# Graph network stack, layer 0: head 0's operands turned on TensorE, part of the adjacency tiles and values moved into the tile loop

## What is computed

```
h = relu(layernorm(x)); Q, K, V = h@Qw+Qb, h@Kw+Kb, h@Vw+Vb        # 512 columns each
S1 = einsum('id,kdh->ikh', Q, A1); S2 = einsum('jd,kdh->jkh', K, A2)
e = S1[i, adj[i,j]] + S2[j, adj[i,j]]                               # per head
attn = softmax(leaky_relu(e, 0.2), axis=1)
x = x + (einsum('ijh,jhd->ihd', attn, V per head).reshape(n, 512) @ Pw + Pb)
```

## Time and profile before

| | before |
|---|---|
| median of 3 runs | 1069.88 us (1066.89 to 1075.04) |
| the profiled execution | 1069.17 us |
| its span in the trace | 1066.9 us |
| TensorE busy | 941.1 us (88%) |
| VectorE / ScalarE / GpSimd busy | 732.8 / 552.6 / 554.4 us |
| mean granted TensorE clock | 0.893 |

### The profile page before, as it was taken

One profiled execution on the slowest core, in us unless ns is written; L12 is line 12 of the kernel. 1 busy time (PEld: TensorE's weight loads), 2 busy tenths in 40 slices (PEclk: granted clock), 3 DMA queues, 4 the chain that ended last, 5 costly groups with the idle time before them and its releaser, 6 DMA issues.

```text
span 1066.9 us, 14476 instructions
## 1 busy us (share of the span) xinstructions
PE 941.1 (88%) x5214; PEld 331.4 (31%) x5214; DVE 732.8 (69%) x1181; ACT 552.6 (52%) x957; POOL 554.4 (52%) x658
## 2 busy tenths in 40 slices
PE   1998999999999999999999379899968949999970
PEld 1853222222222222222224322233332324555430
DVE  3234777777787777877774558611539577999987
ACT  0465666666566665666652047300120138899970
POOL 2005788888989888898781000000000007899962
PEclk8655999999999999999998569999968965999995
DMA  9472011121112112021000000000000000000000
GB/s 197 75 157 73 11 22 63 34 70 35 66 27 67 37 27 74 22 73 33 22 16 7 0 1 1 1 1 1 1 0 1 1 1 0 1 1 1 0 1 20
DMA packets 24764, 32.99 MB, mean 31 GB/s; under 512 B 16187, under 2 KB 16315, under 8 KB 23670
## 3 DMA queue, kind: packets, MB, share of 16 engines
q1 hardware_dynamic: 22390, 23.69, 7.8%
q0 software_dynamic: 2304, 8.39, 4.3%
HBM read 39.17 MB, written 1.29 MB: 38 GB/s over the span
## 4 chain that ended last, share of the span: by engine, by line
PE 74%; DVE 15%; issue 4%; ACT 3%; DMA 2%; POOL 1%; SPq 1%; DVEq 0%; POOLq 0%
PE ps L1102 22%; PE ps L1112 11%; PE ps L1239 8%; PE ps L1089 5%; DVE big L405 4%; PE ps L1081 4%; PE ps L1187 3%; PE ps L1264 3%; PE ps L1300 3%; PE ps L1032 2%; PE ps L993 2%; DVE big L734 2%; DMA big<-in_L_gnn_Pw_dram 2%; DVE big L402 2%; PE ps L1177 2%
## 5 line engine op out<-in xcount | busy, mean ns | idle before, releaser
L538 DVE COPY_PREDICATED big<-mask,ps 128x512 f32<-128x512 uint8 x512 | 338.4, 723 | 109.4 <-PE ps L1089 102.2
L362 POOL TENSOR_SCALAR big<-big 128x512 f32<-128x512 f32 x512 | 355.2, 710 | 67.2 <-PE ps L1112 66.7
L861 ACT ACTIVATE ps<-ps 128x512 f32<-128x512 f32 x512 | 266.8, 583 | 159.8 <-PE ps L1081 159.8
L1102 PE MATMUL ps<-big 128*64 128x512 f32 x1024 | 258.9, 613 | 0.0
L374 POOL TENSOR_TENSOR big<-big 128x512 f32<-128x512 f32 x40 | 67.3, 1682 | 328.7 <-ACT big L939 328.7
L1112 PE MATMUL ps<-big 128*32 128x512 f32 x1024 | 136.3, 604 | 0.0
L1081 PE MATMUL ps<-op_r,op_l 18*128 18x512 bf16 x512 | 109.7, 385 | 1.8 <-DVE mask L530 1.2
L1102 PEld LDWEIGHTS ps<-big 128*64 128x64 f32 x1024 | 58.6, 136 | 135.6 <-issue 98.7
L1300 PE MATMUL ps<-big 66*128 66x512 f32 x160 | 86.1, 667 | 2.2 <-DVE big L707 1.3
L405 DVE TENSOR_TENSOR big<-big,mask 128x512 f32<-128x512 f32 (+1 forms) x72 | 65.8, 933 | 14.8 <-ACT big L881 13.4
L1089 PE MATMUL ps<-op_r,op_l 9*128 9x512 bf16 x512 | 70.6, 389 | 2.0 <-ACT ps L861 2.0
(11 more groups left out here) (242 smaller groups left out, 1139.7 us busy)
## 6 DMA issues: line engine op xcount, KB each, us to landing
big<-in_adj_dram POOLq DMA_DIRECT2D x16, 512.0 KB, 7.7
big<-max_scratch SPq DMA_DIRECT2D x8, 1024.0 KB, 4.9
big<-rden_scratch SPq DMA_DIRECT2D x30, 256.0 KB, 3.3
op_l<-split_scratch SPq DMA_DIRECT2D x64, 36.0 KB
op_r<-split_scratch SPq DMA_DIRECT2D x64, 36.0 KB
x_nat<-in_x_dram SPq DMA_DIRECT2D x1, 512.0 KB, 4.2
out_dram<-x_nat SPq DMA_DIRECT2D x1, 512.0 KB, 3.8
den_scratch<-y_nat SPq DMA_DIRECT2D x30, 8.0 KB
```

Source lines behind the costliest of these rows:

```text
L362: pool.tensor_scalar(ring[:, k % RING, :], vrow[:, head % 2, i0:i0 + HALF], HUGE, g0[:, head, jt:jt + 1], ALU.min, ALU.max).then_inc(s["ba ...
L538: dve.copy_predicated(ring[:, k % RING, :], mask[:, jt, i0:i0 + HALF], ps[:, k % SLOTS, :])\
L861: act.activation(ps[:, k % SLOTS, :], ps[:, k % SLOTS, :], ACT.Relu, scale=-1.0).then_inc(s["relus"], 1)
L1102: m = pe.matmul(ps[w * D:(w + 1) * D, MAIN, :], vp[:, head, jt + w, :], ring[:, (u + w) % RING, :], start=(jt == 0), stop=(jt == NT - 2))
```

## The change

It does five things.

1. **Loads.** GpSimd waits for the weights (w_in, all six loads) before it issues adjacency loads, and issues ten of them up front instead of eight (the last two after layer norm and feature transposes, in buffers that these free). a_rel is read in another order, so that a partition reads 32 neighbouring values and not 8; the transposes of the weights pick their columns to match.
2. **Order of the prologue.** fold comes before the feature transposes. The copies of the turned weights move from VectorE to ScalarE, ahead of its square root for the layer norm; the table set that holds exp and copy is loaded right behind that root.
3. **Work ahead of the loop.** Only 4 of 16 adjacency tiles are turned there (8 half tiles, all copied by ScalarE), and only the values of heads 0 and 1 are made there (4 groups of 4 products with 128 columns).
4. **Head 0's operands.** VectorE puts the 18 rows of head 0 side by side into 32 columns (`slot_l`, `slot_r`), copies them four times across (`wide_l`, `wide_r`, 128 x 2048 bf16 each), TensorE transposes them (32 transposes), and VectorE and ScalarE copy the results straight into op_l and op_r. For head 0 nothing goes through DRAM but the row of m. The split vectors of the other heads go out in one DMA.
5. **The loop.** ORDER puts behind every two tiles one extra, 40 in all: 24 half adjacency tiles (8 transposes each) and then 16 value products of 384 columns (heads 2 to 7). So the first 40 visits hold two tiles and one extra, the others three tiles. The extra uses a PSUM slot; ScalarE copies it in the order of the visit. `select` waits at every 16th tile of head 0 for its part of the mask. GpSimd issues the last six adjacency loads between tiles, and `scale_values` moves from tile 8 of a head to tile 40.

```diff
+        EARLY = 2
-        VISITS = -(-TILES0 // TRIO)
+        LATER = [("adj", n) for n in range(2 * FIRST, 2 * NT)] + [("value", t) for t in range(NT)]
+        for n, extra in enumerate(LATER):
+            ORDER += [("tile", 2 * n), ("tile", 2 * n + 1), extra]
+        ORDER += [("tile", k) for k in range(2 * len(LATER), TILES0)]
+        VISITS = -(-len(ORDER) // TRIO)
+        def crossed_by(v):
+            return 2 * v if v < len(LATER) else TRIO * v - len(LATER)
         def units(v):
-            return min(max(9 * (v - 3) // 4, 0), UNITS)
+            return min(max(3 * (crossed_by(v) - 9) // 4, 0), UNITS)
...
-                sp.dma_start(arel[:, r, :, :], a_rel[r, :, :].rearrange("(c p) h -> p c h", p=P))\
-                    .then_inc(s["a_in"], 16)
+                sp.dma_start(arel[:, r, :, :].rearrange("p (w c) h -> p w c h", w=2),
+                             a_rel[r, :, :].rearrange("(w p c) h -> p w c h", w=2, c=DC)).then_inc(s["a_in"], 16)
...
+        PROLOGUE = [("w", 0), ("fold", 0), ("hT", 0), ("vw", 0), ("s", 0), ("adj", 0), ("adj", 1), ("max", 0), ("adj", 2),
+                    ("max", 1), ("value", 0), ("adj", 3), ("value", 1), ("adj", 4), ("tab", 0), ("value", 2), ("adj", 5),
+                    ("value", 3), ("adj", 6), ("adj", 7), ("split", 0), ("slots", 0)]
...
+            pool.wait_ge(s["w_in"], 16 * 6)
+            for t in range(NHOME - 2):
+                load_adj(t)
+            pool.wait_ge(s["h_ready"], 1)
+            load_adj(NHOME - 2)
+            pool.wait_ge(s["h_turned"], 1)
+            load_adj(NHOME - 1)
...
-            pool.wait_ge(s["adj_turned"], 2 * NT)
+            pool.wait_ge(s["adj_turned"], 2 * FIRST)
...
+            for dst, row, first in ((slot_l, 2, True), (slot_r, 0, False)):
+                for w in range(2):
+                    parts = split[:, (row + w) * H, :, :].rearrange("p c t -> p t c")
+                    dst9 = dst[:, :, w * NINE:(w + 1) * NINE].rearrange("p t (a b) -> p t a b", a=PARTS)
+                    link(dve.tensor_copy(dst9, parts.unsqueeze(3 if first else 2).to_broadcast([P, NT, PARTS, PARTS])))
+            for dst, src in ((wide_l, slot_l), (wide_r, slot_r)):
+                dve.tensor_copy(dst, src.unsqueeze(2).to_broadcast([P, NT, P // SW, SW])).then_inc(s["slots_built"], 1)
+            for b in range(2):
+                dve.wait_ge(s["slots_turned"], b + 1)
+                dve.tensor_copy(op_l[:, 0, b * 2 * HALF:(b + 1) * 2 * HALF], psb[:, b, :]).then_inc(s["slots_in"], 1)
...
+                for kind, k in trio(v):
+                    if kind == "tile":
+                        cross(k)
+                    elif kind == "adj":
+                        turn_adj(k, free_slot("adj", k))
+                    else:
+                        values(k)
```

More of the change, by code:

```diff
@@ L199, in gnn_stack @@
         s = {n: ctx.enter_context(nc.semaphore(n)) for n in names}
-        adj_in = [ctx.enter_context(nc.semaphore(f"adj_in{n}")) for n in range(NADJ)]
+        adj_in = [ctx.enter_context(nc.semaphore(f"adj_in{n}")) for n in range(NHOME)]
         staged = [s["staged0"], s["staged1"]]
@@ L1043, in maxima @@
                         .then_inc(s["mxb"], 1)
-                else:
+            for kind, t in PROLOGUE:
+                if kind == "w":
+                    weights()
+                elif kind == "fold":
+                    fold()
+                elif kind == "hT":
+                    features()
+                elif kind == "vw":
+                    value_weights()
+                elif kind == "s":
+                    score_vectors()
+                elif kind == "adj":
+                    if t >= 4:
+                        pe.wait_ge(s["adj_copied"], t - 3)
+                    turn_adj(t, t % 4)
+                elif kind == "value":
+                    first_values(t)
+                elif kind == "max":
+                    maxima(t)
+                elif kind == "tab":
                     pe.wait_ge(s["tab_ready"], 1)
@@ L1056, in maxima, with free_slot, values @@
                     r.then_inc(s["split_turned"], 1)
-            for kind, t in PROLOGUE:
-                if kind == "adj":
-                    adj_in_rows(t)
-                elif kind == "value":
-                    value_rows(t)
-                elif kind == "max":
-                    maxima(t)
-                elif kind == "hT":
-                    features()
-                elif kind == "fold":
-                    fold()
-                elif kind == "s":
-                    score_vectors()
+                else:
+                    pe.wait_ge(s["adj_copied"], 2 * FIRST)
+                    for bank in range(4):
+                        pe.wait_ge(s["slots_built"], bank // 2 + 1)
+                        for j in range(8):
+                            src = (wide_l, wide_r)[bank // 2][:, bank % 2 * 8 + j, :, :].rearrange("p g r -> p (g r)")
+                            r = pe.transpose(psb[:, bank, j * P:(j + 1) * P], src, identb[:, :])
+                        r.then_inc(s["slots_turned"], 1)
+            TAKEN = {"tile": ("selected", 1), "adj": ("adj_copied", 1), "value": ("vals_read", 1)}
+            def free_slot(kind, k):
+                p = PLACE[kind, k] - SLOTS
+                if p >= 0:
+                    was, n = ORDER[p]
+                    pe.wait_ge(s[TAKEN[was][0]], n + TAKEN[was][1])
+                elif p == 4 - SLOTS:
+                    pe.wait_ge(s["split_copied"], 2)
+                return slot(kind, k)
+            def values(t):
+                pe.matmul(ps[:, free_slot("value", t), 0:(H - EARLY) * D], hT[0:DA, t * P:(t + 1) * P], wv[:, EARLY * D:],
+                          start=True, stop=True).then_inc(s["vals_done"], 1)
             def cross(k):
@@ L1088, in raise_floor @@
                 pe.wait_ge(s["relus"], k + 1)
-                pe.matmul(ps[:, k % SLOTS, :], op_l[g:g + NINE, head % 2, jt * P:(jt + 1) * P],
+                pe.matmul(ps[:, slot("tile", k), :], op_l[g:g + NINE, head % 2, jt * P:(jt + 1) * P],
                           op_r[g:g + NINE, head % 2, i0:i0 + HALF], start=False, stop=True,
```

231 lines of the change are left out of this document (131 added, 100 removed).

## The result

The changed kernel takes 1039.08 us (median of 4 runs, 1037.21 to 1040.50); the kernel before took 1072.46 us beside it (median of 4, 1066.89 to 1075.10). The ratio is 0.975, 95% interval 0.972 to 0.979: faster by 2.5%. On the scale of the median shown ahead of the prediction, the ratio gives 0.9753 x 1069.88 = 1043.4 us. The forecast had the sign and the main mechanism. That it landed inside the range is in part luck: an error in the front and a larger one in the loop have opposite signs, as the part on the prediction shows.

The account below looks back on a forecast made before the run. The loop was taken as bound by TensorE, the first 94 us by waits and dependencies. 1069.2 - 51.5 (front) + 32.6 (loop) = 1050.3 us, stated as 1051 on the median's scale; range 1043 to 1058.

Parts of the forecast that it names:

- Loads: Front: w_in complete near 8.0 us instead of 12.6, a_rel and Pw landed near 10.5 instead of 28.3.
- h: Front, layer norm output: ready at 13.4 us, 0.3 later because ScalarE's square root queues behind the weights' copies.
- The score vectors: Front: TensorE keeps working, so full clock, 3.5 us; their result S is there at 22.4 us (half clock 25.9).
- From S to the exponential: Front, score vectors' result S to exponential: ScalarE's queue is the limit, +7.4 us to its start, +8.3 to its end.
- To the operands: Front, exponential to first cross: 10.9 us, with wide copies at 1.3 each, so the first cross at 41.6 us.
- The row of m: Front: still goes through DRAM, arriving 19 to 24 us after S, possibly delaying the first select; charged 1 us.
- Sum of the front: First cross from 94.1 to 41.6 us, less 1 for m's row: gain 51.5 us, between 44 and 55.
- The loop: TensorE pays 32.6 us: half tiles 10.1, values 13.0, more visits 5.9, start 3.6; bounds 26 to 39.
- two tiles cost the same 0.54: Loop: floors and crosses of a two-tile visit cost as much as for three tiles; 11 more visits add 5.9 us.
- The front gains less: Rival: late weights and a_rel (+5), TensorE at 1.2 GHz throughout (+6); first cross near 52, 1061 us; chance 0.12.
- The extras are hidden: Rival, loop: visits cost nothing more and transposes half, about 17 us paid, 1036 us; chance 0.06.
- The slower one: Rival, loop: ScalarE's copy of the extra delays the relus, 33 us on top, 1084 us; chance 0.08.

Follow-up runs that it names:

- experiment 1: The kernel before with one edit: GpSimd waits for the six weight loads before issuing adjacency loads; 1055.74 us, ratio 0.986.
- experiment 2: The changed kernel without the wait for the weights ahead of its adjacency loads; 1060.98 us, ratio 0.993.
- Experiment 6: The changed kernel with tiles 0 to 79 on two row groups of the array instead of four; 1046.92 us, ratio 0.984.
- experiment 10: The changed kernel with a dummy 128x512 bf16 product on TensorE ahead of each of the 16 score products; 1037.81 us.
- repeated run: The same run as experiment 11: the changed kernel again without any edit; 1036.97 us, ratio 0.968.
- experiment 11: The changed kernel again without any edit, the first of two such repeats; 1036.97 us, ratio 0.968.
- experiment 7: The changed kernel with each of the 24 half tiles in the loop transposed twice; 1046.04 us, ratio 0.982.
- experiment 8: The changed kernel without the loop's 16 value products and their copies, values of heads 2 to 7 constant; 1030.69 us, ratio 0.967.
- experiment 9: The changed kernel with ScalarE's exponential moved ahead of the copy of half tile 3; 1041.01 us.
- experiment 4: The changed kernel with each visit's extra ahead of its two tiles instead of behind them; 1069.98 us, ratio 1.002.

## Why the prediction was right, and where not

**Loads: right; the fold at the lower clock.** w_in is complete at 7.8 (forecast 8.0), the weights' copies at 10.4 (10.7, the square root's line at 10.45 follows them), nothing waits for Pw, and experiments 1 and 2 show that the wait does it. The fold took 3.69 us where I had 1.9. I had halved 3.66 for the clock. In after the fold runs from 10.49 to 14.18, and the clock column reads 1.00 there, but that reading is empty: the trace of after holds no clock value before 18.8 us, and the column then prints 1.00. Experiment 1 shows it in the same 32 products, in two windows of equal length (matmuls of L1010 alone):

```profile
17.70:18.30 0.60, 0.60 (x8) 0.60 (x8) 1.00 1.17 219
...
18.90:19.50 0.60, 0.60 (x13) 0.60 (x13) 1.00 1.10 219
```

They start 0.11 us apart up to 18.3 us, as they do at 0.50 in the kernel before and all through the fold of after, and 0.06 apart from there on, where that trace has its first clock value. At the second pace 32 of them take the 1.9 that I had put. So the halving was right and the level was not: the fold of after ran at 1.2 GHz. Experiment 6 has the same empty column at

```profile
22.00:24.00 2.00, 2.00 (x12) 2.00 (x11) 0.00 (x0) 0.00 (x0) 0.00 (x0) 1.00 1.07 215
```

where its score vectors go at half pace. The mean of 0.66 for the first 94 us counts the first 16.7 as 1.00 in this way, so it is too high. The slow fold cost nothing, as the layer norm covers it; the feature transposes behind it took 3.69 us instead of 3.24, all at the low pace, where the last of those before were faster, and that is within the slack of my sum.

**h: 1.0 us late.** 14.4 instead of 13.4. Forecast was 0.3 for ScalarE's queue. Not seen: the square root pays a table load, as its group ahead of the loop shows in the profile of after,

```profile
L856 ACT ACT_TABLE_LOAD x1 | 1.3, 1283 | 0.0
```

The kernel before had a single load of this kind ahead of the root, at 0.75 us, where nothing waited for it. In after the first load goes with the copies of the weights, now ahead of the root, and the root needs a second one.

**The score vectors: partly wrong.** The step said "here TensorE goes on working, so I take the score vectors at full clock". TensorE did go on working without a gap from 19.66 us, after 0.57 us of waiting, and the clock fell all the same. Windows of after:

```profile
20.00:22.00 2.00, 2.00 (x21) 2.00 (x20) 0.17 (x1) 0.00 (x0) 0.00 (x0) 1.00 1.08 215
22.00:24.00 2.00, 2.00 (x13) 2.00 (x13) 0.00 (x0) 0.00 (x0) 0.00 (x0) 0.55 1.05 213
24.00:26.00 2.00, 2.00 (x19) 1.99 (x19) 1.11 (x2) 0.78 (x1) 0.00 (x0) 0.50 1.07 213
```

A busy share of 2.00 of 2.00 stands beside a clock of 0.55. They took 4.68 instead of 3.5, and S came at 24.3 instead of 22.4: 1.0 from h, 1.2 from the clock, less 0.3 of slack in my sum. In the profile of experiment 10, with other products between these, the clock stayed at 1.00; in that of experiment 1 it did so without them; in experiment 6 it was not up at all, and they took 7.00 us. So what decides it is open. The step that failed is the assumption that TensorE has the full clock as long as it goes on working.

**From S to the exponential: right at full clock, wrong in the profile of after.** I had ScalarE as the limit, +7.4 to its start. In the repeated run, at full clock, it is +7.1. In the profile of after the chain goes through TensorE without a gap from 24.33 to 33.18, half tiles and value products at half clock, and gives +9.9. The half clock was in my range of the gain, at 6 us; against experiment 11 it has cost some 3, and from profile to profile the front varies by 4.8 (first cross at 43.49 to 48.25).

**To the operands: 11.4 for 10.9** (12.4 in the repeated run), but not by the terms I gave. In after the chain goes through TensorE at half clock up to 44.4, not through VectorE. A wide copy takes 0.69 us, not 1.3, unless GpSimd is at work. VectorE's wide copies in the view of one line, of after (minimum/median/maximum in ns, first and last start in us):

```profile
L573 DVE COPY big<-big x2: 695/1544/2392, 40.2 to 40.8; 128x2048 bf16<-128x2048 bf16 x2
```

GpSimd's product of head 0's values and q0 in the timeline of after:

```profile
40.69 2.00 POOL L385 TENSOR_TENSOR big<-big 128x1024 f32<-128x1024 f32 x1 [21.70 <-ACT big L873]
```

The first copy took 0.69; the second began at 40.8, inside GpSimd's product, and took 2.39, ending at 43.2, 0.5 us after it. In the repeated run GpSimd's product comes earlier:

```profile
35.49 1.91 POOL L385 TENSOR_TENSOR big<-big 128x1024 f32<-128x1024 f32 x1 [17.09 <-ACT big L873]
```

and it is the third small copy that takes 1.81 us (the chain above) where the others take 0.25, while both wide copies take 0.69. It is so in all eleven profiles that have these copies: the one copy that starts behind the product's start and ahead of its end is longer by 1.55 to 1.70, and no other is, not even one that starts in the same instant as the product (experiment 7). The Trainium skill ("SBUF — State Buffer", section "SBUF: two separate sides") says that VectorE's faster modes and GpSimd share a pair of ports as an exclusive lock, held for a whole instruction; by that rule the copy should wait for the end of the product, as the trace shows. The Trainium skill's 0.69 for such a copy ("VectorE: DVE Perf Modes", section "Side-by-side: where the cycles go for N=2048 bf16"), which I had cited and not used, agrees with the trace too. In the repeated run the delay is on the path to the first cross; in the profile of after TensorE at half clock covered it. A kernel in which GpSimd's product waits for the slots was not run, so whether it gives back those 1.6 us is open.

**The row of m: hidden.** GpSimd's first tile starts at 42.68, 3.8 ahead of the first cross. I had charged 1 us. In the repeated run it is 1.9 ahead.

**Sum of the front:** 47.6 for 51.5. Of the 4.9 by which the first cross is later than forecast, 1.9 lie before S, 2.4 between S and the end of the exponential, 0.5 behind it; 1.0 comes back from m's row.

**The loop: sizes right, one term with the wrong sign.** Half tiles cost 0.55 (forecast 0.53) and values 0.84 (0.81), and experiments 7 and 8 show that they are paid. The start-up: 57.22 - 46.48 = 10.74 against 7.35, +3.4 (forecast +3.6). There the number is right and the mechanism only in part: I had ScalarE set the pace with 2.1 us a visit, but for most of it the chain goes through TensorE at half clock, 0.94 for the floors and 0.96 for the half tile; ScalarE sets it, with 1.91, where the clock is at 1.00 (experiment 7). That both come to 1.9 is luck. Wrong was the step "two tiles cost the same 0.54". In the chain of after, in visits with values:

```profile
112.87 0.01 PE ps L1188 x2
112.87 0.84 PE ps L1176 x2
```

Two floors and two crosses cost 0.33 to 0.35 together, 0.54 for three of each before. The timeline shows why:

```profile
78.87 0.39 PE L1196 MATMUL ps<-op_r,op_l 9*128 9x512 bf16 x2
...
78.88 0.39 PE L1188 MATMUL ps<-op_r,op_l 18*128 18x512 bf16 x2
```

All four products start together. I had seen that products on different row groups run side by side, but only within a group of floors or crosses, and not that two and two make four. The Trainium skill ("TensorE: Matmul & The Clock Gate", section "Why this matters for your kernels") says that products with few rows, each on row groups of its own, run concurrently; experiment 6 agrees, with 8.6 us. So the 35 paid visits of the new kind cost 35 x 0.34 = 11.9, where 71 / 3 = 23.7 visits of the old kind cost 12.8: -0.9 for a forecast of +5.9. This is 6.8 of the 9.3 us by which the loop came out cheaper. Another 0.9 is that all aggregates now come in pairs, 1.87 for two, where a third of them had stood alone at 1.01. The remaining 1.6, net of the 0.8 by which half tiles and values came out dearer, are the half clock at the loop's start (3.15 for the first unit of eight, 3.61 in the chain of before) and the two ends of the stretch, and were not taken apart.

**Behind the loop: -4.2, which I had not expected.** No code changed there. In the chain the 16 products of before L1147 take 3.53 us and those of after L1257 take 1.85, half clock against full. In the other kernels this stretch lasts from 486.9 to 492.2 us with the same code: 492 in experiments 6 and 9, which have the change, and 488.1 in experiment 1, which has not. So it is no gain of the change. That it depends on where the clock falls is argued from such rows; no experiment was made for it. The 4.2 us are the chance of two single profiles, one of before and one of after.

**The rivals.** "The front gains less" came true by two fifths of its size, 3.9 of 10 us. "The extras are hidden" gave 1036, near the time measured, but by a mechanism that did not occur. The slower one did not occur, and experiment 4 shows how near it was: one swap in a list. What kept it away is the order in ScalarE's queue, relus first, so that its copies lie beside TensorE's units.

Against the forecast for the profiled execution, 1050.3, the measured 1040.5 is 9.8 less: 3.9 more for the front, 9.3 less for the loop, 4.2 less behind it, 0.2 outside the span. So the front's error hid a part of the loop's. My range had allowed 26 us for the loop at least, "no visit cost", because it held a cost below nothing to be excluded. That bound was the mistake: the row that I used for a visit with three tiles could not show what one with two costs.

## What to carry to other kernels

Where small products on different row groups follow each other, count the groups over all neighbouring instructions, not within one kind: how many tiles make a visit decides whether the second kind is free. Where a copy is moved into a loop of an engine in order, put it behind what the next stage waits for; here that order is worth as much as the whole change. And check what a new order of loads delays before counting what it brings: one small load that all work hangs on cost 20 us behind the large ones. Ahead of the first clock value of a trace, compare the pace of equal products before trusting the column.

## What the runs showed of the hardware

- The granted clock fell from 1.00 to 0.55 in a stretch in which TensorE had no gap (22 to 24 us, in the first profile of after and in the first repeated run). From there the same code ran at half clock until 42 us in the one, and at full clock again from 26 to 32 in the other; that goes with a first cross 3.0 us earlier. In experiment 6 TensorE was busy without a gap from 19.1 to 34.9 us, and its score vectors and transposes kept the pace of the lower level throughout.
- Small products (128 x 65 weights, 8 columns) start 0.11 us apart at granted clock 0.50 and 0.06 apart at 1.00: 32 take 3.66 us in the kernel before, and 2.17 in experiment 1, where the pace changed on the way.
- The clock column of a window reads 1.00 where the trace has no clock value yet (up to 18.8 us in after, 16.7 in before, 43.7 in experiment 6), whatever the pace of the products.
- A bf16 copy of VectorE from SBUF that starts during a GpSimd product with two SBUF operands ends 0.1 to 0.6 us behind that product: 1.81 for 0.25, 2.39 for 0.69. Selects that start inside such a product keep their 0.72 to 0.75 us, and a copy out of PSUM in the kernel before its 1.22.
- A second round of 8 transposes into the same bank costs 0.45 where the first costs 0.55.
- Two products of 9 rows and two of 18, on four row groups, start within 0.01 us and end 0.39 us later.
